# Packing the adjacency bits of layer 0: weights and moving side exchanged, two chunks a run

## The reference, cut to what matters

```python
h = jnp.maximum(_layernorm(x, axis=-1), 0.0)
Wh = h @ W                                         # 8192 x 128
e = leaky_relu((Wh @ a1)[:, None] + (Wh @ a2)[None, :])
attention = softmax(jnp.where(adj > 0, e, NEG), axis=1)
x = x + attention @ Wh                             # layers 1 to 3 put an elu or a threshold around it
```

## Time and profile before

| | before |
|---|---|
| median of 3 runs | 3875.64 us (3874.84 to 3876.75) |
| profiled execution, span from first to last instruction | 3874.5 us |
| TensorE busy with matmuls | 3813.1 us, 98% |
| VectorE busy | 3570.8 us, 92% |
| ScalarE busy | 1226.2 us, 32% |
| one group of the sweep in layer 0, from TensorE's first matmul to that of the next | 61.62 us |
| one group in layer 1 | 58.08 us |

### The profile page before, as it was taken

The page is one execution under the profiler, slowest core; times in us unless marked ns, Lnnn a source line. Parts: engine busy times, 40 slices in busy tenths (PEclk is TensorE's granted clock), DMA queues, the critical chain, the costliest instruction groups (busy, mean ns, idle before and its releaser), DMA issues.

```text
span 3874.5 us, 83734 instructions
## 1 busy us (share of the span) xinstructions
PE 3813.1 (98%) x35495; PEld 3804.2 (98%) x35495; DVE 3570.8 (92%) x7790; ACT 1226.2 (32%) x2553; POOL 17.0 (0%) x107
## 2 busy tenths in 40 slices
PE   7999999999999999999999999999997999999999
PEld 6999999999999999999999999999997999999999
DVE  7988989888899999999999999999997999999998
ACT  6777777777631111111133121121122000000000
POOL 1000000000000000000000000000000000000000
PEclk9999999999999999999999999999998999999999
DMA  7888888888400100000002000000000000000000
GB/s 236 294 294 292 293 289 293 286 290 295 142 18 20 18 20 20 18 20 20 15 15 67 17 20 20 18 20 20 18 18 12 17 12 17 15 12 17 15 16 11
DMA packets 222983, 343.96 MB, mean 89 GB/s; under 512 B 72464, under 2 KB 147344, under 8 KB 222608
## 3 DMA queue, kind: packets, MB, share of 16 engines
q1 hardware_dynamic: 220880, 338.35, 27.8%
q10 hardware_dynamic: 1728, 0.27, 0.0%
HBM read 305.57 MB, written 21.20 MB: 84 GB/s over the span
## 4 chain that ended last, share of the span: by engine, by line
PE 96%; ACT 2%; DVE 1%; DMA 1%; issue 0%; ACTq 0%; SPq 0%; DVEq 0%
PE acc L1242 93%; PE ps_pack L1156 1%; PE ps_wh L1260 1%; ACT vals L1438 1%; ACT adj_pairs L1343 0%; DMA vals<-in_x_dram 0%; PE acc L1224 0%; DVE q L782 0%; PE ps_bc L1200 0%; DMA adj_int<-in_adj_dram 0%; DVE mask L755 0%; PE acc L1179 0%; ACT e L1363 0%; ACT wh L1369 0%; DMA rrow<-rows 0%
## 5 line engine op out<-in xcount | busy, mean ns | idle before, releaser
L1242 PE MATMUL acc<-vals,q 128*128 128x129 f32 (+1 forms) x32576 | 3669.7, 275 | 5.2 <-DVE q L782 5.0
L1242 PEld LDWEIGHTS acc<-vals,q 128*128 128x128 f32 x32576 | 3653.0, 192 | 6.9 <-issue 5.2
L782 DVE SCALAR_TENSOR_TENSOR q<-rrow,R,mask 128x512 f32<-128x512 f32 x3968 | 2829.1, 748 | 165.4 <-PE acc L1242 20.9
L1343 ACT ACTIVATE adj_pairs<-adj_int,threshold 128x1024 uint8<-128x1024 int32 x512 | 585.3, 1146 | 223.2 <-PE ps_pack L1156 155.7
L755 DVE TENSOR_SCALAR mask<-bits 128x512 uint16<-128x512 uint16 x2048 | 437.8, 292 | 7.6 <-DMA rrow<-rows 4.7
L1450 ACT ACTIVATE xnew<-acc,rec 128x128 f32<-128x128 f32 x244 | 69.2, 365 | 855.8 <-DVE rec L820 761.0
L1457 ACT ACTIVATE e<-xnew 128x512 f32<-128x512 f32 x47 | 29.6, 631 | 405.0 <-DVE xnew L851 317.3
L1470 ACT ACTIVATE e<-xnew,nm,rs 128x128 f32<-128x128 f32 x193 | 79.6, 482 | 220.9 <-DVE nm L627 220.9
L1523 ACT ACTIVATE wh<-ps_wh 128x512 f32<-128x512 f32 x48 | 28.7, 598 | 336.9 <-PE ps_wh L1260 336.0
L1465 ACT ACTIVATE sd<-ve 128x4 f32<-128x4 f32 (+1 forms) x49 | 9.9, 202 | 365.4 <-DVE ve L608 365.4
L851 DVE SCALAR_TENSOR_TENSOR xnew<-mean,none,xnew 128x128 f32<-128x128 f32 x188 | 65.2, 347 | 51.6 <-ACT xnew L1450 51.6
(11 more groups left out here) (230 smaller groups left out, 736.0 us busy)
## 6 DMA issues: line engine op xcount, KB each, us to landing
adj_int<-in_adj_dram SPq DMA_DIRECT2D x512, 512.0 KB, 4.9
rrow<-rows SPq DMA_DIRECT2D x60, 256.0 KB, 3.3
x_between_layers<-xnew SPq DMA_DIRECT2D x32, 256.0 KB, 4.0
xin<-x_between_layers SPq DMA_DIRECT2D x32, 256.0 KB, 2.8
xin<-in_x_dram SPq DMA_DIRECT2D x16, 256.0 KB, 5.5
wh_of_layer<-wh SPq DMA_DIRECT2D x1, 4096.0 KB, 16.8
x_of_layer<-xnew SPq DMA_DIRECT2D x16, 256.0 KB, 2.3
xin<-x_of_layer SPq DMA_DIRECT2D x16, 256.0 KB, 2.7
```

The source lines that it names most:

```text
L782: nc.vector.scalar_tensor_tensor(q[:, j % RING, :], row, column(R_, t), mask[:, c % 2, j, :], ALU.max, ALU.mult).then_inc(q_ready, 1)
L1242: last = nc.tensor.matmul(to, q[:, j % RING, b * P:(b + 1) * P], vals[:, t, 0:width(g.layer)], start=first, stop=(t == KT - 1 or g.two and ...
L1343: nc.scalar.activation(adj_bytes[:, n % BIN_RING // 2, :, n % 2], adj_int[:, n % ADJ_RING, :], ACT.Sign, bias=threshold[:, 0:1], accum_out ...
```

## The change

For the pieces 120 to 455 (`FROM_4`, `TO_14`; groups 3 to 13) the pack is turned round: `packer` (128x32) is the weights, and a pair of pieces is the moving side, 256 columns a matmul. The four column blocks b of a pair go to PSUM partitions 32b to 32b+31, four quarters of the columns of the array. A run packs two chunks, 16 pieces, with 32 such matmuls into `ps_pack` and `ps_bc`; there are 21 runs for 42 packs. They stand behind tiles 26 and 60 of a group (`RUNS_AT`). The result lies transposed, so ScalarE copies it to a buffer (`copy_words`, two copies) and one DMA transpose a run (`turn_words`) writes the words to `bits`; VectorE's `unpack` waits for that DMA. Four more pairs are buffered, in the part of `bits` that belongs to the last two groups. The stream of pieces is shifted by `STREAM`: eight more pieces in group 2, eight fewer in group 13; the single packs of groups 1 and 2 stand 14 tiles apart instead of 16 (`single_at`). The lists of ScalarE and SP get new places for the other work (`SIGNS_AND_OUTPUTS`, `TRANSFERS`). Packs before piece 120 and from 456 on stay as they were, 22 of 64.

```diff
+FROM_4, TO_14 = 120, 456
+RUN = 2 * QP
+RUNS_AT = (26, 60)
+STREAM = [LEAD * QP, 48, 80] + [PIECES * g + 24 for g in range(3, LAST - 1)] + [464, 496, 512]
+SIGNS_AND_OUTPUTS = {1: (7, 18, 21, 27, 32), 2: (9, 22, 26, 32, 40), "run": (5, 16, 19, 26, 32), "one": (7, 18, 21, 27, 30)}
+TRANSFERS = {1: (12, 22, 25, 27), 2: (14, 26, 30, 32), "run": (12, 17, 23, 25), "one": (12, 22, 25, 27)}
...
+def single_at(C):
+
+    if C <= FROM_4 // QP:
+        return 64 + (C - 6) * 14 + 13
+    return (C - 1) * JC - 1
...
+def buffer_of_pair(G):
+
+    pair = G // 2
+    return (pair - FROM_4 // 2) % BIN_RING if in_run(G) else pair % (BIN_RING // 2)
...
+            def turn_words(G):
+                n = (G - FROM_4) // RUN + 1
+                sp.wait_ge(words_copied, 2 * n)
+                sp.dma_start_transpose(all_words[:, G // QP * JC * WORDS:(G // QP + 2) * JC * WORDS]
+                                       .rearrange("p (n r) -> p n r", r=P), words_of_run).then_inc(words_turned, 16)
...
+                    if i < len(pieces):
+                        G = pieces[i]
+                        if in_run(G - RUN - ADJ_RING) and (G - FROM_4) % RUN == ADJ_RING:
+                            turn_words(G - RUN - ADJ_RING)
+                        load_piece(G)
...
+                    if in_run(C * QP):
+                        dve.wait_ge(words_turned, 16 * ((C * QP - FROM_4) // RUN + 1))
...
+            def pack_run(G0):
+
+                if G0 == FROM_4:
+                    pe.wait_ge(bits_ready, FROM_4 // QP)
+                need(pe, words_copied, (G0 - FROM_4) // QP)
+                pe.wait_ge(adj_binary, G0 + RUN)
+                for i in range(0, RUN, 2):
+                    r = buffer_of_pair(G0 + i)
+                    pairs = adj_pairs[:, r, :] if r < BIN_RING // 2 else spare_pairs[:, r - BIN_RING // 2, :]
+                    pairs = pairs.rearrange("p (k b c) -> p k b c", k=2, b=BLOCKS)
+                    to, half = (ps_pack, ps_bc)[i // QP], i % QP // BLOCKS
+                    for b in range(BLOCKS):
+                        last = nc.tensor.matmul(to[b * WORDS:(b + 1) * WORDS, half * 2 * P:(half + 1) * 2 * P],
+                                                packer[:, i % BLOCKS // 2, :], pairs[:, :, b, :],
+                                                start=(i % BLOCKS == 0), stop=(i % BLOCKS == 2), skip_group_check=True)
                     last.then_inc(adj_packed, 2)
...
+                        if t in RUNS_AT:
+                            G0 = (g.value * CHUNKS + (3, 5)[RUNS_AT.index(t)]) * QP
+                            if in_run(G0):
+                                pack_run(G0)
...
+            def copy_words(G0):
+
+                act.wait_ge(adj_packed, G0 + RUN)
+                for a, ps_ in enumerate((ps_pack, ps_bc)):
+                    nc.scalar.activation(words_of_run[:, a * JC * WORDS:(a + 1) * JC * WORDS], ps_[:, :], ACT.Copy,
+                                         scale=2.0 ** 24).then_inc(words_copied, 1)
```

More of the change, by code:

```diff
@@ L111, in tile, with in_run, kind, pieces_of @@
         return self.into if self.unit else slice(self.value * BLOCKS + b, self.value * BLOCKS + b + 1)
+def in_run(G):
+    return FROM_4 <= G < TO_14
+def kind(g):
+    return g.value if g.value in (1, 2) else "run" if FROM_4 <= STREAM[g.value] < TO_14 else "one"
+def pieces_of(g):
+    return range(STREAM[g.value], STREAM[g.value + 1])
+def buffer_of_pair(G):
+    pair = G // 2
+    return (pair - FROM_4 // 2) % BIN_RING if in_run(G) else pair % (BIN_RING // 2)
+def freed_by(G):
+    pair, ring = G // 2, BIN_RING // 2
+    if in_run(G):
+        first = pair - FROM_4 // 2 < BIN_RING
+        if first and buffer_of_pair(G) >= ring:
+            return 0
+        before = pair - ring if first else pair - BIN_RING
+    else:
+        before = pair - BIN_RING if 0 <= G - TO_14 < 2 * ring else pair - ring
+    return 2 * (before + 1)
+def singles_before(C):
+    return C if C * QP < FROM_4 else C - (TO_14 - FROM_4) // QP
 class Steps:
@@ L318, in build @@
         bits_ready = sem("bits_ready")
+        words_copied = sem("words_copied")
+        words_turned = sem("words_turned")
         degree_ready = sem("degree_ready")
@@ L1246, in chunk @@
                         pack(*FIRST_PACKS[t])
-                    if g.layer == 0 and g.value > 0 and j == JC - 1 and ahead(g.value, c)[0] <= LAST:
-                        pack(*ahead(g.value, c))
+                    if g.layer == 0 and g.value > 0:
+                        for C in range(5, CHUNKS * GROUPS):
+                            if not in_run(C * QP) and single_at(C) == g.value * KT + t and C > 5:
+                                pack(C // CHUNKS, C % CHUNKS)
+                        if t in RUNS_AT:
+                            G0 = (g.value * CHUNKS + (3, 5)[RUNS_AT.index(t)]) * QP
+                            if in_run(G0):
+                                pack_run(G0)
                     between(t)
@@ L1528, in outputs_of @@
             def outputs_of(g, due):
-                due.append((QP - 1, lambda: scaled_sums(g)))
+                by = kind(Rows(0, g.value + 1)) if g.layer == 0 and g.value < LAST else "one"
+                summed, deviated, normal, turned_back, projected_ = SIGNS_AND_OUTPUTS[by]
+                due.append((summed, lambda: scaled_sums(g)))
                 if g.layer > 0:
@@ L1532, in outputs_of @@
                 if g.layer < 3:
[L1533 to L1536 removed]
+                    due.append((deviated, lambda: deviations(g)))
+                    due.append((normal, lambda: normalised(g)))
+                    due.append((turned_back, lambda: copy_hT(g)))
+                    due.append((projected_, lambda: copy_wh(g)))
             def sweep(g, before):
```

94 lines of the change are left out of this document (56 added, 38 removed).

## The result

The changed kernel takes 3892.21 us (median of 5 runs, 3890.99 to 3895.82), the kernel before 3875.79 us on the same chip: ratio 1.0043, interval 1.0032 to 1.0053, 16.4 us slower.

A forecast was written before the change was run, and what follows sets the result against it. TensorE's matmul stream, 98% busy, was taken as the bound. Packs removed -37.2, runs +24.2, single packs +6 and late run pieces +5 gave -2.0 us, so 3873.6 us; range 3862 to 3896 us.

The forecast's parts named there:

- Packs and runs on TensorE: TensorE in layer 0: 42 packs removed at 0.885 us, 21 runs added at 1.15 us; balance -13.0 us without waits.
- Quarters side by side: Inside a run: four array quarters overlap, giving eight rounds of 0.11 = 0.89 us.
- Rival 3: Runs on TensorE: quarters don't overlap, 3.7 us a run, +43 us, about 3919 us; chance 0.12.
- Single packs of groups 1 and 2: Packs every 14 tiles: TensorE waits up to 3.8 us behind tile 41 of group 1; together 2 to 9 us, taken +6.
- The runs' pieces: Groups 3 to 12: 16 pieces late for runs by 0.5 us a group, 0 to 1.2; +5 us in all.
- The walk: Step through groups 3 to 12, landings 5.0 us: 1.2 us spare at tile 26, tile 60 on time or 0.1 late.
- rival 2: Supply of pieces becomes the bound, at the tile 60 run: landings 5.5 us, +21 us, about 3897 us; chance 0.18.
- The price from which it decides: Groups 3 to 12: slower once a group's runs are late by more than 0.7 us together, 7 us over ten groups.
- Hidden: ScalarE's copies, VectorE's wait for turned words and SP's wait for copied words were claimed to cost no time.
- covers: If ScalarE reached the copies late, hiding of VectorE's and SP's waits would go, and loads behind SP's wait with it.

The follow-up runs named there:

- The fastest experiment: Changed kernel with eight piece buffers, ScalarE's normalised rows and SyncE's halves transpose and input rows later, words' transpose still four pieces behind its run: 3867.20 us.
- the ring of eight: Changed kernel with eight piece buffers instead of four up to piece 327, words' transpose issued eight pieces behind its run instead of four: 3897.81 us, ratio 1.006.
- the transfers moved alone: Changed kernel, four buffers, with only SyncE's transpose of halves two pieces later and next input rows four pieces later: 3902.22 us, ratio 1.0067.

## Why the prediction failed, point by point

- **Packs and runs on TensorE: right.** A group without lateness takes 60.44 us, as forecast, so a run costs (60.44 - 58.08) / 2 = 1.18 us where I took 1.15. 21 runs are +24.8 us against the 37.2 removed: -12.4, forecast as -13.0. The fastest experiment brings 8.0 us of it.
- **Quarters side by side: right.** The two halves of a run start 0.44 us apart, so each round of four matmuls takes 0.11 us. Rival 3 is out.
- **Single packs of groups 1 and 2: the place was right, the sum mis-sized.** +6 forecast, +11.65 measured. The idle time is 6.3 us of it. The other 5.35 us are busy time: 4.5 us are two stretches of 112 matmuls at the lower clock (15.59 and 14.39 us instead of 12.75), which no term held; most of the rest are packs cut in two by a wait. The wait came where I put it (tile 41 of group 1, 0.50 and 1.90 us), and at packs of group 2 besides.
- **The runs' pieces: this step failed.** 0.5 us a group forecast, bounded at 1.2, against 1.6 measured: +16.15 instead of +5. The walk had the wait for `nm`, at 33.3 us (it came at 33.7 in group 6), and gave every load behind it 5.0 us to land. It named the transpose and the input rows in front of three loads and then put a few tenths on them. Measured are 6.1 and 6.2 us at the median for two of these loads (7.4 and 7.5 in group 6), 1.1 us and more above the 5.0 that I used; as the walk had the run on time to 0.1 us, it all counts, and the run at tile 60 is late by 1.3 us on average (some 13 of the 16 us; 3 are at tile 26). The trace of the kernel before could have told me: its first load behind the input rows takes 6.1 us, too. Nor did I see that SyncE's own stand at the halves and ScalarE's order each hold the fourth buffer.
- **The outcome is rival 2's**, in the place that it named (tile 60) and for most of its size (16.4 of 21 us), but with another split (16.15 us at the runs and 11.65 at the single packs, where it had 25 and 9) and without its cause: the landing stayed at 5.1 us at the median, and what was late were the few loads that mattered. The price from which it decides was lower than the 0.7 us a group that I gave: with 11.65 us lost in groups 1 and 2, only 0.8 us were left of the balance.
- **Hidden: right in the changed kernel.** No wait of VectorE for turned words stands in groups 3 to 12, and its wait of 3.27 us for the sums is gone. SyncE stands 45.1 us at the copied words in ten groups, and as foretold it costs little: in group 6 the load behind starts at 474.79, the piece that frees its buffer was signed at 474.5. The sentence that covers would go if something came between was shown the hard way by the ring of eight.

What stays open: how the few long landings divide between the row transfers ahead of them and the clump of loads itself; no run took the input rows away. Why the transfers moved alone lost 10 us and not nothing. And which waits lower the clock and which don't.

## What to carry to other kernels

Fewer, larger gatherings of pieces turn slack that lies between small ones into a deadline: what counts is no longer the share of time in which the supply is idle, but whether the last piece is there. So walk the supply at its worst place with the landing of the loads that stand behind other transfers, which the trace has, not with the median of all, and look at what every in-order queue stands in front of while a buffer is free. Where two conditions each hold the same resource, undoing one can show nothing; test them together before calling either innocent. And price a stall of TensorE as more than its length.

## What the runs showed of the hardware

- A matmul of 32 weight columns and 256 columns lasts 273 ns at the median and its weight load 97 ns by their own rows; 32 such pairs, four quarters in turn, take 0.98 us together, less than a third of what the matmuls' 256 columns would take one after the other (32 x 0.107 = 3.4 us), so matmuls and weight loads of different quarters overlap although all use the same 128 rows:

```profile
L1253 PEld LDWEIGHTS ps_bc<-bits,packer x336: 96/97/97, 286.5 to 907.9; 128*32 128x32 f16 x168
L1253 PE MATMUL ps_bc<-bits,packer x336: 272/273/273, 286.7 to 908.0; 128*32 128x256 f16 x168
```

- The Trainium skill ("TensorE: Matmul & The Clock Gate", Part 3, The mechanism) says in one line that a weight load overlaps a matmul in flight only where the row groups differ; these rows speak against it, and for the gain from column tiles that the same part lists. Its drain at a change of the tiling ("TensorEngine Tiling (Array Packing)", Key Properties) can be no more than small: 1.18 us less eight rounds of 0.11 leaves 0.3 us for both edges of a run together.
- A granted clock of 0.50 followed a wait of 2.5 us in group 2, which cost 2.8 us beside the wait, and waits of 0.5 and 1.9 us close together in group 1, which cost 1.6 us; none followed one of 2.6 us in group 6.
- The landing time of a load grew with the loads under way, 5.1 us at the median of ten groups with four buffers, 5.8 (own buffers) and 7.0 (lent ones) with six up to piece 343, 7.4 and 7.2 in the fastest kernel, with eight up to piece 327, at 297, 300 and 303 GB/s: more loads in flight bought earlier starts and hardly more bandwidth.
